# Attention and the last expert stage in one block, expert tiles ahead of the shared jobs, low halves by VectorE

## The reference, cut to what matters

```python
def _L1_ffn_ref(hidden_states, norm_weight, router_w, sw1, sb1, sw2, sb2, ew1, eb1, ew2, eb2):
    var = jnp.mean(jnp.square(hidden_states), axis=-1, keepdims=True)
    normed = hidden_states * jax.lax.rsqrt(var + 1e-08) * norm_weight
    shared = jnp.maximum(normed @ sw1 + sb1, 0.0) @ sw2 + sb2
    ...
    probs = jax.nn.sigmoid(flat @ router_w.T)
    scores, idx = jax.lax.top_k(probs, TOPK)
    w = scores / (jnp.sum(scores, axis=-1, keepdims=True) + 1e-06)
    ...
    h = jnp.maximum(jnp.einsum('td,edh->teh', flat, ew1) + eb1[None, :, :], 0.0)
    eo = jnp.einsum('teh,eho->teo', h, ew2) + eb2[None, :, :]
    routed = jnp.einsum('teo,te->to', eo, comb)
    return shared + routed.reshape(b, s, -1)
x = x + _L1_xattn_ref(_layernorm(x, axis=-1), ctx_2048, ...)
x = x + _L1_ffn_ref(_layernorm(x, axis=-1), ...)
```

## Time and profile before

| | us |
|---|---|
| median of 3 runs | 1444.42 (1444.32 to 1447.08) |
| span of the profiled execution, its own time | 1468.5 |
| TensorE busy in it | 1250.4 (85%) |
| VectorE busy | 1054.3 (72%) |
| ScalarE busy | 899.3 (61%) |
| GpSimd busy | 653.5 (44%) |

### The profile page before, as it was taken

The page is one execution under the profiler, slowest core; times in us unless marked ns, Lnnn a source line. Parts: engine busy times, 40 slices in busy tenths (PEclk is TensorE's granted clock), DMA queues, the critical chain, the costliest instruction groups (busy, mean ns, idle before and its releaser), DMA issues. The chain is left out here.

```text
span 1468.5 us, 35946 instructions
## 1 busy us (share of the span) xinstructions
PE 1250.4 (85%) x13401; PEld 1041.2 (71%) x13401; DVE 1054.3 (72%) x2080; ACT 899.3 (61%) x1699; POOL 653.5 (44%) x677
## 2 busy tenths in 40 slices
PE   4999998399999999997599999999997268999880
PEld 3777777278777877786489888888886256787660
DVE  5888888566877687675256678989887369676563
ACT  3888887566565666654355655666654248787660
POOL 2222222145655555564332345556755327165561
PEclk9999999689999999999699999999999669999995
DMA  4222221332213221321210000000000123146646
GB/s 143 93 94 93 94 93 64 116 94 80 73 39 92 80 73 37 94 80 44 86 38 17 10 17 9 17 15 18 24 13 17 44 58 89 48 151 217 203 139 182
DMA packets 88373, 109.64 MB, mean 75 GB/s; under 512 B 13322, under 2 KB 55050, under 8 KB 88202
## 3 DMA queue, kind: packets, MB, share of 16 engines
q1 hardware_dynamic: 83210, 97.05, 21.3%
q0 software_dynamic: 4992, 10.30, 2.1%
HBM read 61.70 MB, written 29.82 MB: 62 GB/s over the span
## 5 line engine op out<-in xcount | busy, mean ns | idle before, releaser
L830 POOL TENSOR_TENSOR b_h_lo<-b_h,b_h_hi 128x512 fp32r<-128x512 f32 x168 | 216.3, 1292 | 179.7 <-ACT b_h_hi L854 179.2
L849 ACT ACTIVATE b_zg<-b_zg 128x512 f32<-128x512 f32 x168 | 97.6, 581 | 82.0 <-PE b_zg L894 81.8
L854 ACT ACTIVATE b_h_hi<-b_h 128x512 fp32r<-128x512 f32 x168 | 105.2, 626 | 65.7 <-DVE b_h L1059 65.6
L1059 DVE TENSOR_TENSOR b_h<-b_zg,b_uw 128x512 f32<-128x512 f32 x168 | 116.2, 692 | 32.1 <-ACT b_zg L849 26.8
L2173 POOL DMA_INDIRECT planes_dram<-d_y_out,d_back x92 | 94.5, 1028 | 93.6 <-DVE d_y_out L2484 68.8
L1052 DVE TENSOR_TENSOR b_uw<-b_zu,b_gw 128x512 f32<-128x512 f32 x128 | 88.2, 689 | 57.7 <-PE b_zu L894 50.9
L2453 DVE TENSOR_TENSOR d_h_lo<-d_h,d_h_hi 128x512 fp32r<-128x512 f32 x124 | 85.1, 689 | 44.6 <-ACT d_h_hi L2214 26.8
L312 POOL TENSOR_TENSOR a_qx<-a_qT,headmask 128x256 f32<-128x256 f32 x64 | 37.9, 612 | 150.3 <-ACT a_qT L347 150.3
L519 DVE TENSOR_REDUCE a_top<-a_score_ps 128x8 f32<-128x1024 f32 x64 | 78.1, 1220 | 18.6 <-PE a_score_ps L410 18.6
L1293 POOL TENSOR_TENSOR c_prob<-c_prob,c_recip 128x512 f32<-128x512 f32 x64 | 65.5, 1044 | 50.9 <-DVE c_recip L1709 50.9
L1716 DVE TENSOR_TENSOR c_oT_lo<-c_oy,c_oT_hi 128x512 fp32r<-128x512 f32 x64 | 43.7, 683 | 58.1 <-ACT c_oT_hi L1421 57.5
(11 more groups left out here) (393 smaller groups left out, 4172.3 us busy)
## 6 DMA issues: line engine op xcount, KB each, us to landing
rows_dram<-a_blank SPq DMA_DIRECT2D x32, 520.0 KB, 3.3
b_gw<-gates_dram SPq DMA_DIRECT2D x64, 256.0 KB, 3.9
d_up_slot<-d_up_tab SPq DMA_DIRECT2D x15, 512.0 KB
d_down_slot<-d_down_tab SPq DMA_DIRECT2D x15, 512.0 KB
d_xg<-rows_dram SPq DMA_DIRECT2D x23, 260.0 KB
b_gm<-gates_dram SPq DMA_DIRECT2D x32, 160.0 KB, 3.8
c_craw<-in_c_ctxT_dram SPq DMA_DIRECT2D x16, 256.0 KB, 3.1
d_pay<-planes_dram SPq DMA_DIRECT2D x12, 256.0 KB, 4.3
```

The costliest lines, as they stand in the source:

```text
L830: pool.tensor_tensor(h_lo[:, m % HS, :], h[:, m % HF, :], h_hi[:, m % HS, :].bitcast(F32), ALU.subtract).then_inc(lo_done.sem, 1)
L849: act.activation(zg_ps[:, n % ZG, :], zg_ps[:, n % ZG, :], ACT.Silu).then_inc(sg_done.sem, 1)
L854: act.activation(h_hi[:, m % HS, :], h[:, m % HF, :], ACT.Copy).then_inc(hi_done.sem, 1)
L1059: dve.tensor_tensor(h[:, n % HF, :], zg_ps[:, n % ZG, :], uw[:, n % 2, :], ALU.mult).then_inc(h_done.sem, 1)
```

## The change

`attention1` and `sorted_experts` no longer have a block each. Each engine's part of either is a generator, and `in_turn` draws from both: 39 ticks of attention alone (ScalarE 38), then 16 times one tick of attention and one step of the last stage, then what is left of attention and then the rest. All 8 groups are routed in attention's ticks, which now run to 49, and the last stage has no router. The first 18 steps of the last stage split one weight piece each, and `nth` is larger than the number of pieces, so no low half is GpSimd's. The jobs come in the order 23 tiles, then 8 shared jobs. The planes are fetched into buffers of their own for all groups, GpSimd adds the two planes of a group, and VectorE adds the sum to x between its steps of the last jobs. The memory of attention is given to the last stage piece by piece, with waits on attention's marks.

```diff
@@ attention1 @@
-        ticks = range(-6, UNITS + 8)
+    ticks = range(-6, UNITS + 18)
...
-            return g if odd == 0 and 0 <= g < ROUTED else None
+        return g if odd == 0 and 0 <= g < GROUPS else None
...
-                    if g is not None and g + 1 < ROUTED:
+                if g is not None:
                         scatter(g, lo, hi)
@@ sorted_experts @@
-    JOBS = GROUPS + TILES
+    JOBS = TILES + GROUPS
...
-        weights = SplitWeights(nc, ctx, tag + "sw", jobs, 3)
+    weights = SplitWeights(nc, ctx, tag + "sw", jobs, len(jobs) + 1, sw_raw)
...
+    def join_step(g):
+        return divmod(CH * (TILES + 4) + 1 + 2 * g, CH)
...
+    def sync(sp):
+        sp.wait_ge(marks["q_made"].sem, marks["q_made"].at(2 * UNITS))
+        sp.wait_ge(marks["k_made"].sem, marks["k_made"].at(2 * UNITS))
+        weights.sync(sp, 0, 1)
...
+        weights.sync(sp, 1, len(jobs))
...
+                    for g in range(GROUPS - 2, GROUPS):
+                        wait_rows(sp, g)
...
+    def gpsimd(pool):
...
+        for g in range(GROUPS):
+            pool.wait_ge(fetched[g], 32)
+            pool.tensor_tensor(plane(g, 0), plane(g, 0), plane(g, 1), ALU.add).then_inc(joined.sem, 1)
...
+    def vector(dve):
...
+            for g in range(GROUPS):
+                if (k, c) == join_step(g):
+                    tiles = x[:, g * GROUP:(g + 1) * GROUP, :]
+                    dve.wait_ge(joined.sem, joined.at(g + 1))
...
+                    dve.tensor_tensor(tiles, tiles, plane(g, 0), ALU.add).then_inc(summed.sem, 1)
@@ second_half, new @@
+        alone = 39
+        order = [(0, 1), (1, 1)] * 16 + [(0, 2), (1, 500)]
...
+        @block.scalar
+        def _(act):
+            in_turn([(0, alone - 1)] + order, first.scalar(act), second.scalar(act))
@@ new @@
+def in_turn(order, first, second):
+    stages = (first, second)
+    for which, steps in order:
+        for _ in range(steps):
+            next(stages[which], None)
```

More of the change, by code:

```diff
@@ L20 @@
 from contextlib import ExitStack, contextmanager
+from collections import namedtuple
 from itertools import product
@@ new lines, in sorted_experts @@
+    up_in, down_in = ([sem(f"{n}_in{s}") for s in range(WS)] for n in ("up", "down"))
+    stored, summed = sem("stored"), tally("summed")
+    fetched = [sem(f"fetched{g}") for g in range(GROUPS)]
+    joined = tally("joined")
+    added = [sem(f"added{s}") for s in range(2)]
+    jobs = []
+    for e in [*range(1, E + 1), 0]:
+        for m, (shared, name) in enumerate(((up_shared, "d_w"), (down_shared, "d_wd"))):
+            row = tab[:, e - 1, m, :] if e else shared[:, :]
+            jobs += pieces(row[:, 0:half], row[:, half:W], a[name][:, e * half:(e + 1) * half])
@@ L2144, in _ @@
-            for g in range(GROUPS):
-                sp.wait_ge(summed.sem, summed.at(2 * g + 2))
-                if g + PAY < GROUPS:
-                    fetch(g + PAY)
-                sp.dma_start(out[g * COLS:(g + 1) * COLS, :].rearrange("(u p) f -> p u f", p=P),
-                             x[:, g * GROUP:(g + 1) * GROUP, :]).then_inc(stored, 16)
-            sp.wait_ge(stored, 16 * GROUPS)
+            in_turn([(0, alone)] + order, first.sync(sp), second.sync(sp))
         @block.gpsimd
@@ L2177, in _ @@
-            for i in range(2 * GROUP):
-                u, n = divmod(i, 2)
-                pool.indirect_dma_start(rows, bass.IndirectOffsetOnAxis(ap=route.dest[:, n, u:u + 1], axis=0),
-                                        route.pay[:, n, u, :], None).then_inc(scattered_last, 16)
-            ticks(step)
+            in_turn([(0, alone)] + order, first.gpsimd(pool), second.gpsimd(pool))
         @block.scalar
         def _(act):
-            for m in (xhi_done, twin_done, sig_done, h_act, hi_done, y_done):
-                m.credit(act)
@@ L2331, in _ @@
[L2331 removed]
+            in_turn([(0, alone)] + order, first.tensor(pe), second.tensor(pe))
         @block.vector
         def _(dve):
[L2335 to L2345 removed]
@@ L2498, in _ @@
-            ticks(step)
-            for g in range(GROUPS):
-                tiles = x[:, g * GROUP:(g + 1) * GROUP, :]
-                dve.wait_ge(fetched[g % PAY], 32 * (g // PAY + 1))
-                for n in range(2):
-                    dve.tensor_tensor(tiles, tiles, pay[g % PAY][:, n, :, 0:C], ALU.add).then_inc(summed.sem, 1)
-                    if n == 0:
-                        dve.wait_ge(summed.sem, summed.at(2 * g + 1))
+            in_turn([(0, alone)] + order, first.vector(dve), second.vector(dve))
@@ L2508, in program @@
+    earlier.sems = [s for s in earlier.sems if s not in finished]
 def program(nc, a, rows, gates, planes, out):
```

2291 lines of the change are left out of this document (1088 added, 1203 removed).

## The result

The changed kernel takes 1464.27 us, median of 4 runs (1463.93 to 1465.02), where the kernel before takes 1445.56 (1444.32 to 1447.08): a ratio of 1.0125, 95% interval 1.0108 to 1.0142 (the ratio is worked out from all runs, here and below, and is not the quotient of the medians; the two differ by up to 0.22%). By the medians it is 18.7 us slower; the forecast was 1439 and faster, and the range of 1427 to 1454 does not hold it.

What follows compares the result with a forecast made beforehand. Bound by TensorE, 85% busy, with two holes, mid-kernel and at the end. Tail -34.6, jobs -28.8 and drain +57.8 sum to -5.6 us on the profiled 1468.5, scaled to -5.5 on the runs: 1439 us, range 1427 to 1454.

Steps and rivals of the forecast that it cites:

- The runs' median of 1444.42 is 0.984 of that, so -5.5: Last step of the sum: scales -5.6 us on the profiled 1468.5 to the runs, giving 1439 us.
- I keep the 13.0 us of stalls: In the jobs' term: 13.0 us of stalls over the 6.40 us pace stay, since the slot copies stay.
- Rival 1: Much faster: gaps in the drain and tiles do not come back, 1439 - 11 = 1428 us; chance 0.22.
- the drain: Attention's end, all 8 groups routed there: GpSimd's serial chain lengthens, first `d_z` 1240.5 against 1182.73, +57.8 us.
- 1142.55: Clock time of before's tick from which GpSimd's drain work was counted: 71.6 us plus 19.1 to the last scatter.
- the first wait: GpSimd's wait ahead of group 4's scatters in the drain, for VectorE's statistics, variance, low half and probabilities: 4.6 us.
- the last two: Waits ahead of group 6's and 7's scatters, for landing and fill of the one payload buffer: 6.7 and 4.6 us.
- the second: Wait ahead of group 5's scatters, for group 4's landing, then fill, load, exponential and probabilities: 1.9 us.
- the jobs: First `d_z` to last `d_y_sb`, 31 jobs: 242.6 us before, 213.8 after with stalls kept, -28.8 us.
- rival 3: Slower: GpSimd's eight joins hold VectorE in the shared jobs, 10.2 us, plus 6 in the drain: 1454 us; chance 0.12.
- the tail: Kernel's end: scatters, fetches and sums hidden under 8 shared jobs, 43.2 us behind the last job become 8.6, -34.6 us.
- The low halves: 18 weight pieces by VectorE, 16 in the drain's ticks: cost nothing, and GpSimd's six (1.27 us each) are saved.

Runs made afterwards that it cites:

- ahead2: Changed kernel with two payload buffers and two of eight shared jobs ahead of the tiles, behind routing's last tick: 1464.79 us, ratio 0.9981; run again, 1440.79 us, 0.9953.
- two_pay: Changed kernel with two buffers for the payload and two for the destinations in place of one: 1482.20 us, ratio to before 1.0098.
- after_again: The changed kernel, unchanged, run again beside the kernel before on one chip: 1483.11 us, ratio to before 1.0126.
- dve_joins: Changed kernel with GpSimd's eight adds of the planes made by VectorE, just ahead of each join: 1483.28 us, ratio to before 1.0141.
- small_after: Changed kernel with weight copies into slots cut to 128 of 1024 columns for 12 of 15 tiles (wrong weights): 1483.45 us, ratio to before 1.0117.

## Why the prediction was wrong

**The step that failed** is the last: "The runs' median of 1444.42 is 0.984 of that, so -5.5". The profiled execution stood 24 us above the runs because it had gaps and they had none; the changed kernel's sum of 1462.9 us was scaled down by 23.9 us that no run of it could give back. With gaps, side by side, before takes 1463.2 us and the changed kernel 1483.1; without, 1445.6 and 1464.3. The ratio is 1.0126 and 1.0125. The profile said that the two numbers did not belong together, and the text treated the difference as a factor. This rests on the changed kernel and ahead2, seen both ways; no run has a profile of before without gaps.

**"I keep the 13.0 us of stalls"** failed with it. The stalls were the gaps' and are absent in the profile of the changed kernel; before's 242.6 us of jobs held them too. Rival 1 named this and put it on the change alone, when it belongs to both kernels.

**The terms**, measured in the profile without gaps, from marks that the prediction set. Its sum without the 13.0 would have been 1462.9 - 13.0 = 1449.9; the span is 1462.1. The 12.2 us:

- the drain, mis-sized by 4.6 by the clock. From its scaling at 1140.87, the place that 1142.55 marks in before, to the last scatter the changed kernel takes 96.2 us, forecast 90.7; the 5.5 are the waits, 23.0 in place of 17.8, and small change. It starts 1.7 earlier, and loses 0.8 from the last scatter to the first `d_z` (8.0 against 7.2). The mechanism was right for the first wait, which the text gave to VectorE's chain and which a second buffer leaves at 5.0, and for the last two, which two_pay shows to be the one buffer's. It was wrong for the second, 3.8 in place of 1.9, which hangs on VectorE and not on the fill;
- the jobs, 208.5 us against 200.8 without stalls: 4.7 (27.5 against 22.8) is the last four, where adds, joins and a normalise meet. That is rival 3's place, and its mechanism, GpSimd's adds holding VectorE, is there; but the sum stays at 27.5 where VectorE adds, so the cost is that of all this work on a full VectorE. The text named it, priced it at 10.2 and cost it at nothing in the sum, on a share of 72%, a mean that says nothing of a job with a normalise and a join. Nor does 72% give its 4.6 us of 6.4: 112.67 us over 23 jobs are 4.9. 2.3 is the second period (8.65 us) and 0.9 the start (first copy 12.5 us after the first `d_z`, forecast 11.6);
- the tail was right: 8.4 us behind the last copy, forecast 8.6.

Added up, 4.6 + 7.7 - 0.2 give the 12.2, but for rounding. Stalls kept by mistake (13.0) and terms too small (12.2) nearly cancelled, by luck, so that last copy (1453.67, forecast 1454) and span (1462.1, 1462.9) came out as foretold. A sum that agrees so well with its trace was still wrong on the time.

**A term put at nothing** lies ahead of all this. The forecast counts from before's 1142.55 as if nothing changed up to there. From the scaling of the first group to this one, the three profiles of before take 299.8, 299.3 and 299.8 us; after_again, dve_joins and two_pay, with gaps like them, 303.8, 303.9 and 304.1. So the change costs some 4 us there. Group 5's first products now lie in that stretch; that they cost it is not shown. In the profile without gaps the changed kernel takes 299.5, which hides it beside before's profile with gaps.

**Taken without gaps on both sides**, the forecast would have been near no change. The 1449.9 still has before's gaps ahead of 1142.55 in it: 4 to 5 us, an estimate from the changed kernel and ahead2, whose same stretch is 4.3 and 5.3 us longer with gaps than without. That makes 1445 to 1446, and with 1.9 around the span 1447 to 1448 against 1445.6, where the forecast had -5.5. The sign hung on the gaps; the other 16 to 17 of the 18.7 us are the terms too small: 5.5 + 0.8 in the drain, 7.7 in the jobs, and some 3 to 4 ahead of the drain.

**The low halves** were costed at nothing beside what GpSimd saves. For the changed kernel the run with a third on GpSimd leans the same way (4.7 us, not clear of noise).

## What to carry to other kernels

When the profiled execution is longer than the runs, find the microseconds in the trace before using them: take out what waits for nothing of the kernel's, from both kernels, and sum against the runs. A serial drain of one engine is best filled with work that no engine of its chain must do in between: two shared jobs behind the last tick are worth their 12.8 us (1.0098 to 0.9981 against two_pay), four between the ticks gained nothing that the runs show (1.0073). And an engine's share over a stretch doesn't price an addition; the fullest job of it does.

## What was not expected of the hardware

One program on one chip took 1464.8 us in one set and 1440.8 in another, with 29 us more in the first profile than in the second, where no row has "remote"; before went from 1468.8 to 1447.9 with it. With 12 of 15 tiles' copies cut to an eighth there were still such rows (12.1 us in small_after). What drives them is open.

A four-row normalise of VectorE (`d_xn`) took 1.11 us alone, 2.08 and 3.15 beside GpSimd's adds of 1.3 to 1.8 us, and `d_h_lo` 0.68 alone and 1.77 beside one. A `c_raw` of 128x32 took 0.19 us alone, 1.4 beside one product of GpSimd and 3.99 beside two. The Trainium skill (SBUF — State Buffer, "Who interferes with whom") has it that a VectorE instruction with two SBUF inputs contends with a GpSimd instruction that reads SBUF; `d_h_lo` agrees. The same section of the Trainium skill also counts `tensor_scalar`, which `d_xn` is, among the operations that can contend with GpSimd, when its operands meet the conditions of a mode with two ports; `d_xn` agrees with that, and no run shows which mode it was in.
